# An adaLN block with linear attention and routed experts on one core: the ranking of a token group one head sooner, and the hand-over to the expert phase rearranged

## The reference

```python
def attn(x, w_qkv, w_out, b_out, proj):          # 4 x 1024 tokens, width 128, 8 heads of 16
    q, k, v = split(x @ w_qkv.T)                  # in blocks of 32 tokens
    qp = elu(q @ proj) + 1;  kp = elu(k @ proj) + 1      # 128 features for each head
    kv = kp.T @ v
    out = (qp @ kv) / (qp @ kp.sum(tokens) + 1e-8)       # within each block
    return out @ w_out.T + b_out

def ffn(x, w_red, wg, w1, b1, w2, b2):            # 8 experts, hidden width 512
    gates = softmax((x @ w_red) @ normalised(wg).T)
    idx, score = argmax(gates), max(gates)
    return (gelu(x @ w1[idx] + b1[idx]) @ w2[idx] + b2[idx]) * score

sa, ca, ga, sb, cb, gb = rows of silu(c) @ wmod          # ga, gb kept away from 0
h = layernorm(x) * (1 + ca) + sa;  x = x + ga * attn(h, ...)
h = layernorm(x) * (1 + cb) + sb;  x = x + gb * ffn(h, ...)
```

## Time and profile before

| | |
|---|---|
| three runs | 324.13, 325.55, 326.32 us, median 325.55 |
| profiled execution | 321.42 us, of which the span from the first to the last instruction is 319.7 |
| busy share of the span | PE 86%, DVE 74%, ACT 70%, POOL 49% |
| granted TensorE clock, mean | 0.949 of full speed |

### The profile page before, as it was taken

The page is one execution under the profiler, slowest core; times in us unless marked ns, Lnnn a source line. Parts: engine busy times, 40 slices in busy tenths (PEclk is TensorE's granted clock), DMA queues, the critical chain, the costliest instruction groups (busy, mean ns, idle before and its releaser), DMA issues. The chain is left out here.

```text
span 319.7 us, 11500 instructions
## 1 busy us (share of the span) xinstructions
PE 275.4 (86%) x4012; PEld 222.2 (70%) x4013; DVE 236.5 (74%) x769; ACT 224.2 (70%) x510; POOL 158.0 (49%) x173
## 2 busy tenths in 40 slices
PE   8789799999999999999999977684949699999960
PEld 3555577777777677687677756574849599999950
DVE  2767969989979989899899999595523456666740
ACT  1377788999889799889898689364237276676730
POOL 7104144362684774755746804557743434455550
PEclk9999999999999999999999999898578899999995
DMA  5996000000010011010100205134954424444400
GB/s 148 322 333 181 0 3 4 2 2 4 4 51 27 28 51 51 29 51 28 50 28 29 76 27 152 49 102 126 243 148 121 109 67 126 119 124 108 125 22 0
DMA packets 16240, 26.16 MB, mean 82 GB/s; under 512 B 2607, under 2 KB 11059, under 8 KB 16192
## 3 DMA queue, kind: packets, MB, share of 16 engines
q1 hardware_dynamic: 12464, 16.50, 18.8%
q0 software_dynamic: 3296, 8.41, 7.7%
q10 hardware_dynamic: 432, 0.59, 0.6%
HBM read 15.32 MB, written 10.64 MB: 81 GB/s over the span
## 5 line engine op out<-in xcount | busy, mean ns | idle before, releaser
L1129 DVE SCALAR_TENSOR_TENSOR phi<-ps,ebuf 128x512 f32<-128x512 f32 x128 | 82.0, 682 | 17.9 <-ACT ebuf L540 17.4
L536 ACT ACTIVATE ebuf<-ps 128x1024 f32<-128x1024 f32 x64 | 65.6, 1026 | 16.4 <-PE ps L766 15.6
L540 ACT ACTIVATE ebuf<-ebuf 128x512 f32<-128x512 f32 x128 | 74.4, 636 | 0.1
L764 PE MATMUL ps<-hT_hi,mix_lo 128*128 128x512 f32 x128 | 58.4, 456 | 8.2 <-DVE phi L1129 4.9
L594 ACT ACTIVATE gT<-ps,b_cols 128x128 f32<-128x128 f32 x156 | 44.7, 368 | 19.8 <-issue 13.6
L866 PE MATMUL ps<-w_sb,gT 128*128 x312 | 45.9, 294 | 13.2 <-DVE y L1446 11.3
L866 PEld LDWEIGHTS ps<-w_sb,gT 128*128 128x128 f32 x312 | 41.2, 206 | 15.2 <-issue 15.2
L766 PE MATMUL ps<-hT_hi,mix_hi 128*128 128x512 f32 x128 | 50.6, 396 | 0.0
L765 PE MATMUL ps<-hT_lo,mix_hi 128*128 128x512 f32 x128 | 50.6, 395 | 0.0
L495 POOL DMA_INDIRECT out<-yo,tok x27 | 27.4, 1014 | 29.7 <-issue 15.9
L446 POOL DMA_INDIRECT sorted_rows<-rec,pos x32 | 33.0, 1030 | 8.8 <-issue 5.4
(11 more groups left out here) (197 smaller groups left out, 452.5 us busy)
## 6 DMA issues: line engine op xcount, KB each, us to landing
rin<-sorted_rows SPq DMA_DIRECT2D x39, 192.5 KB
w1b<-in_L_ffn_w SPq DMA_DIRECT2D x1, 2048.0 KB, 14.2
sorted_rows<-pad_rec SPq DMA_DIRECT2D x6, 192.5 KB
sorted_rows<-pad_rec ACTq DMA_DIRECT2D x3, 192.5 KB
w1b<-in_L_ffn_b SPq DMA_DIRECT2D x1, 512.0 KB, 6.0
sorted_rows<-rec,pos POOLq DMA_INDIRECT x32
out<-yo,tok POOLq DMA_INDIRECT x27
wmod_sb<-in_L_wmod SPq DMA_DIRECT2D x1, 384.0 KB, 3.5
```

What stands on the lines that cost most here:

```text
L536: nc.scalar.activation(ebuf[:, h % 2, :, :], x_ps[h % 2], ACT.Relu, scale=-1.0).then_inc(s_neg, 1)
L540: nc.scalar.activation(ebuf[:, h % 2, j, :], ebuf[:, h % 2, j, :], ACT.Exp, scale=-1.0).then_inc(s_exp, 1)
L764: mm(x_ps[h % 2][:, j, :], mix_lo[:, j, h, :], hi, start=True, stop=False)
L1129: v.scalar_tensor_tensor(out=phi[:, h % 4, j, :], in0=x_ps[h % 2][:, j, :], scalar=0.0, in1=ebuf[:, h % 2, j, :], op0=ALU.max, op1=ALU.add ...
```

## The change

The ranking of group g-2 moves from head 7 to head 6 of step g, and for groups 0 to 5 into unused columns of PSUM bank 6, which `apply_values` of half 0 writes too. So it no longer waits for the residual (`s_x2`), the turning of the next group no longer waits for `s_pos`, and `apply_values` of half 0 waits for `s_cr` instead. In the last step the ranking of group 5 stands in head 5, the exponential of its gate in head 4, its score in head 5 and its positions in head 6. POOL scatters tile 0 of group 5 at the end of the last step and the other three one by one behind it. SP reads the row numbers of slots 12 to 17 one at a time, each just before or after a fetch. SP writes six paddings instead of five, and ACT two instead of three and one slot later. DVE adds the bias of slot 3 before the scores and positions of group 7 instead of behind them.

```diff
-    PADS_SP = E - 3
+    PADS_SP = E - 2
...
+        def rank_of(g):
+            return m_ps if isinstance(g, int) and g >= NG - 2 else ps[:, 6, TG * NC * VW:512]
...  (SP)
-            rows = [row_of(s) for s in range(EARLY, EARLY + RING)]
+            row = row_of(EARLY)
             sp.wait_ge(s_tail, 16 * (E + 1))
...
-            for s, row in zip(range(EARLY, EARLY + RING), rows):
+            for s in range(EARLY, EARLY + RING):
                 sp.wait_ge(f_yd, s - RING + 1)
                 fetch(s, row)
+                if s + 1 < EARLY + RING:
+                    row = row_of(s + 1)
...  (POOL)
                 if prev2:
                     build_scale(g - 2, firstp2)
+                if is_last(g):
+                    scatter(g - 2, [0])
                 if prev:
                     pool.wait_ge(s_ln2, 3 * g)
                     rsqrt(ln2_rs[:, :], ln2_ve[:, :], s_rs2)
...
             residual_base(NG - 1, False)
-            scatter(NG - 3, [0, 1])
+            scatter(NG - 3, [1])
             norm2_scale(NG - 2, False)
+            scatter(NG - 3, [2])
             pool.wait_ge(s_ln2, 3 * NG)
             rsqrt(ln2_rs[:, :], ln2_ve[:, :], s_rs2)
-            scatter(NG - 3, [2, 3])
+            scatter(NG - 3, [3])
...  (ACT)
-                    if h == 5 and prev2:
+                    if h == (4 if is_last(g) else 5) and prev2:
                         gate_exp(g - 2)
...
             gelu(5, 1)
-            act.wait_ge(s_table, 1)
-            for e in range(PADS_SP, E):
-                pad_region(act, e)
             for s in range(RING + 1, EARLY):
                 take_early(s)
                 keep_in(s, s)
                 gelu(s - 1, (s - 1) % 2)
+                if s == RING + 1:
+                    act.wait_ge(s_table, 1)
+                    for e in range(PADS_SP, E):
+                        pad_region(act, e)
...  (PE)
-                if is_last(g) and half == 1:
-                    pe.wait_ge(s_cr, NG - 1)
-                elif not first:
+                if half == 0 and g >= 2:
+                    pe.wait_ge(s_cr, g if g < NG - 1 else NG - 1)
+                if not first and not (is_last(g) and half == 1):
                     pe.wait_ge(s_on, 2 * g + half)
...
+                    if h == 5 and is_last(g):
+                        rank(g - 2)
...
-                    if h == 7 and prev2:
-                        pe.wait_ge(s_x2, g)
+                    if h == 6 and prev2 and not is_last(g):
                         rank(g - 2)
...  (DVE)
+                    if h == 5 and is_last(g):
+                        score_sum(g - 2)
+                        score_inverse(g - 2, firstp2)
...
+                        if h == 6:
+                            position_rows(NG - 3)
+                            position_own(NG - 3)
+                            position_sum(NG - 3)
+                            position_out(NG - 3, False)
...
+            add_bias(3, 3)
             scale_add(2, 2, 0)
             score_sum(NG - 1)
...
             position_out(NG - 1, False)
-            add_bias(3, 3)
```

More of the change, by code:

```diff
@@ L823, in rank @@
                 pe.wait_ge(s_pick, g + 1)
+                at = rank_of(g)
                 for t in range(TG):
                     for u in range(t + 1):
-                        mm(m_ps[:, t * E:(t + 1) * E], before[:, :] if u == t else ones_b[:, :], pick[:, u, :],
+                        mm(at[:, t * E:(t + 1) * E], before[:, :] if u == t else ones_b[:, :], pick[:, u, :],
                            start=(u == 0), stop=(u == t))
                 for t in range(TG):
-                    last = mm(m_ps[:, TG * E:(TG + 1) * E], ones_b[:, :], pick[:, t, :], start=(t == 0), stop=(t == TG - 1))
+                    last = mm(at[:, TG * E:(TG + 1) * E], ones_b[:, :], pick[:, t, :], start=(t == 0), stop=(t == TG - 1))
                 last.then_inc(s_rk, 1)
@@ L908, in step @@
                     if h == 2 and prev2:
-                        if not (isinstance(g, int) and g == 2):
-                            pe.wait_ge(s_pos, g - 2)
                         pe.wait_ge(s_x2, g - 1)
@@ L1258, in position_rows @@
                 dve.wait_ge(s_cr, g + 1)
-                v.tensor_tensor(posf[:, :, :], m_ps[:, 0:TG * E].rearrange("p (t e) -> p t e", e=E),
+                v.tensor_tensor(posf[:, :, :], rank_of(g)[:, 0:TG * E].rearrange("p (t e) -> p t e", e=E),
                                 carry[:, :].unsqueeze(1).broadcast_to([P, TG, E]), ALU.add).then_inc(s_ps, 1)
@@ L1264, in position_own @@
                 dve.wait_ge(s_ps, 2 * g + 1)
-                v.tensor_tensor(carry[:, :], m_ps[:, TG * E:(TG + 1) * E], carry[:, :], ALU.add).then_inc(s_cr, 1)
+                v.tensor_tensor(carry[:, :], rank_of(g)[:, TG * E:(TG + 1) * E], carry[:, :], ALU.add).then_inc(s_cr, 1)
                 v.tensor_tensor(posr3[:, :, :], posf[:, :, :], pick[:, :, :], ALU.mult).then_inc(s_ps, 1)
@@ L1318, in last_head @@
             def last_head():
-                position_rows(NG - 3)
-                position_own(NG - 3)
                 normalise_sum(NG - 1, 0)
-                position_sum(NG - 3)
                 normalise_inverse(NG - 1, 0)
-                position_out(NG - 3, False)
                 normalise_out(NG - 1, 0)
@@ L1388, in step @@
                         split_hi(g + 1, False)
+                    if h == 5 and is_last(g):
+                        score_sum(g - 2)
+                        score_inverse(g - 2, firstp2)
                     if h == 6:
-                        if prev2:
+                        if prev2 and not is_last(g):
                             score_sum(g - 2)
```

## The result

Four runs of the changed kernel took 328.89, 329.05, 329.49 and 333.00 us (median 329.27), four of the kernel before beside them 324.09 to 326.32 (median 324.84). The ratio is 1.018, 95% interval 1.013 to 1.023: slower by 4 to 7.5 us. The profiled execution took 329.49 us (span 327.7), 8.0 above the profiled one of before; the median difference is smaller since that execution of before was a quick one, as the prediction says.

The account below looks back on a forecast made before the run. The prediction saw a nearly full ring of PE, DVE and ACT, then SP's list in the hand-over. Terms 3.6 + 1.5 + 1.5 = +6.6 us on the median 325.55 gave 332, range 324 to 336.5.

Parts of the forecast that it names:

- part 1: Steps 3 to 7: PE waits 1.3 us for `carry` before half 0; 0.9 a step, +3.6 us (1.6 to 6.5).
- part 2: Last step: ranking of group 5 waits 2.8 us for `pick`; +1.5 us at the last count (0.5 to 4.3).
- the hand-over: Last count to the late slots: SP's sixth padding delays slot 9's fetch, +1.5 us (1.0 to 2.2).
- rival B: Ring absorbs the wait: part 1 at 1.6, perhaps part 2 low too; 329 to 330, or 328; chance 0.18.
- the ring: First-phase steps: PE, DVE and ACT hand work round, nearly full; PE leaves 0.9 us of a 22.3 us step.
- Rival D: Last step: PE's 2.8 us standstill could halve the clock, up to +1.7 us, 333.7; counted within the forecast's 0.46.
- Part 3: Hand-over: a sixth padding on SP before slot 9's fetch, +1.5 us (1.0 to 2.2).
- rival C: Queues get fuller: ACT stands 2 x 2.2 us for its paddings, part 2 nearer its upper end; +11, 336.5; chance 0.12.
- Part 4: Hand-over: earlier bias of slot 3, single row loads, sooner copy of slot 7's weights; at nothing, covered by SP's list.
- Rival A: Hand-over becomes quick: six paddings in 7.0 us, SP reaches slot 9 within 8 us; 325 or 322; chance 0.24.

Follow-up runs that it names:

- part 1 alone: Kernel before with only the steady steps' ranking in bank 6 and head 6, and half 0 of the applied values waiting for `carry`; ratio 1.0106.
- the trace of part 3: Kernel before with only six paddings on SP, two on ACT behind slot 7's gelu, and late slots' row numbers loaded one by one; ratio 0.997.
- parts 3 and 4 together: Kernel before with paddings 6 and 2, row numbers one by one, and slot 3's bias ahead of the last group's positions; ratio 1.0005.
- the repaired kernel: The whole change with group 5's ranking behind head 5's projection and scores, its positions at head 5's end; ratio 1.0075 against the kernel before.
- parts 3 and 4 each alone: Two runs on the kernel before: paddings 6 and 2 with row numbers one by one, 0.997; slot 3's bias ahead of the last positions, 1.0009.
- the outputs held back: Kernel before with POOL's output DMAs of the twelve early slots each waiting for a later slot than their own; ratio 0.9997.
- held back and spaced: Kernel before with early outputs held until all paddings landed and a small POOL operation of some 1.05 us behind each; ratio 1.0101.

## Why the prediction held, and where it did not

The direction and the range held: 332 was forecast, in 324 to 336.5, and 329.27 measured. That the sum came near is in part luck: between the two profiles it was +6.6 forecast and +8.0 measured, with part 1 1.6 too high, part 2 2.8 and the hand-over 1.2 too low, and 1.0 gained at start and end that nothing forecast. The measured time even lies just outside the forecast's own 329.5 to 335, in the 329 to 330 of rival B; of B the half on part 1 came true (+2.0 for its 1.6), the low end of part 2 did not. Point by point:

- **Part 1, the mechanism right, the size too large.** The wait came at the forecast place (1.37 for 1.3), and a step grew by 0.5, near the low end of 0.4, not by 0.9: +2.0 for four steps instead of +3.6. Of PE's 1.37 the ring swallowed 0.9, about PE's spare time in a step in the earlier trace rows. I had followed the delay only to DVE's head 2 and called the rest gapless; its gaps there were enough.
- **Part 1, the failed step.** "In the fifth, the last step, ACT waits 2.54 us [...] and that covers it" looked at step 7's first half 0. The same line of `apply_values` also runs for the last group behind head 7, where the wait is for `carry` of group 5. With part 1 alone PE stood there for 3.10 us, in the whole change for 1.26.
- **Part 2, undersized: +1.5 taken, +4.3 came**, the range's own upper end. The wait for `pick` (2.67 for 2.8) and DVE's wait for ACT (3.10 for 2.9) came as forecast. What I took off again did not: I counted on the 2.76 "remote" wait before the last sum to swallow the delay, and in its place stands a 2.67 wait for PE; PE itself ended late, by the half clock behind the first stop and by the second wait. Rival D's clock (up to +1.7) was real, about 3.5 us at half speed, and should have stood in the sum. The reason given for leaving it out was a misreading: the gap ahead of the slow window of the earlier trace rows was 2.57 us, not longer than the forecast stop of 2.8. A slip of the sum beside it: 3.4 less 2.76 leaves 0.64, not 0.9.
- **Part 3, the size plausible, the cause wrong.** I priced the sixth padding at 1.5 us between ACT's and SP's rows. Alone, it costs nothing. The Trainium skill ("DMA: Bandwidth & Descriptors", on issuing engines not being separate queues) has the split save only sequencer time; the trace of part 3 agrees in that the transfers cost the same, and even the sequencer's time did not show, since SP stood anyway. Of my two bounds the 2.2 was taken from SP under the hold-up and the 1.0 from ACT, which issued freely; neither was the price of one more padding in a list whose length the hold-up sets. That the queues were full, as the prediction reads these rows, is not what they show: ACT issued its two in 1.45 us while SP's were slow. So rival C's stand of ACT for 2 x 2.2 us did not come either.
- **Part 4, "at nothing", failed in company.** The earlier bias lets a sixth output be ready, which lengthens POOL's row by 1.3 us. With the sixth padding behind the row's end the late slots start 2.7 us later (3.0 in parts 3 and 4 together), but only 0.9 later in the repaired kernel, which has both parts too. By the times of parts 3 and 4 this cost at most 1.2.
- **Rival A** needed slot 9 within 8 us of the last count; it took 16.6. The quick list that it described exists (6.67 us for five paddings), but it needs POOL's outputs out of the way, and nothing in the change does that.

The parts add up: 1.06, 1.31 and 0.05 per cent make 2.4 where 1.8 was measured, within the intervals; by stretches of the trace +2.0, +4.3 and +2.7, less 1.0 at start and end, make the 8.0 of the two profiles.

## What to carry to other kernels

A wait that is added for a shared bank has to be looked up at every place where its line runs, the first and last iteration above all, and priced together with the list behind it: here the same ranking cost 1.3% ahead of the projection and nothing two places later. When several engines are released in the same microsecond by nothing that the profile names, look for a third engine whose row of DMAs ends just then, before pricing what they were waiting to do. Rows of indirect DMAs without a gap were worth breaking up here, but only from the start: held-back work came back as a row beside the late slots.

## What the runs showed of the hardware

- **Indirect DMAs in a row hold up the other engines.** While POOL issued them every 1.28 us (0.97 busy, 0.30 gap), SP's paddings took 2.2 us apiece, and signals of PE's finished work reached DVE and ACT late: DVE waited 7.67 us in before for an outer layer that PE had ended 6.1 us earlier, ACT 7.74 us in after. Rows of nine and ten ended at 234.71 and 241.93; SP was free at 236.1 and 243.6, DVE and ACT 1.5 to 2.0 us after the row's end. With one every 2.3 us (gap 1.3) behind the scatters the paddings took 1.4 apiece; with the four scatters alone, 1.3. In the late slots one every 2.0 us does no visible harm; eight in a row cost 9 us. How far SP gets before it slows down varies: behind the same row of nine the fetch of slot 9 came 13.9 to 14.1 us after the last count in four kernels with five paddings, and 15.0 in a fifth. The Trainium skill ("Perfetto Trace Analysis", section on the DMA instruction of GpSimd) says that such an instruction's end in the profile is the end of writing its descriptors, not of moving data; no row here shows where between the two the others are held, and no run tried a gap between 0.3 and 1.3 us.
- **The clock after a short stop is not the same from run to run.** Behind the same stop of PE (2.6 us before 204.3 and 204.7) matmuls went at half the clock for about 3.4 us in before and for about 10 us in the kernel with parts 3 and 4: granted clock by windows

```profile
210.00:215.00 5.00, 3.98 (x45) 3.69 (x45) 4.37 (x19) 3.56 (x13) 2.52 (x4) 1.00 0.46 129
```

```profile
210.00:215.00 5.00, 5.00 (x25) 5.00 (x25) 3.08 (x12) 2.07 (x8) 1.89 (x2) 0.50 0.39 122
```

(before above, parts 3 and 4 below; the clock is the third figure from the end). The last step came out at 48.6 and 50.7 us, and the whole difference arises between the `carry` of group 5 and that of group 6 (16.7 and 18.8 us), where the clock differs. It is the same in the other kernels with that stop: 3.4 us at half the clock and 16.7 in parts 3 and 4 each alone, 10 us and 18.8 with the outputs held back, and with them held back and spaced. Why one execution gets its clock back sooner stays open; parts 3 and 4 each alone were run on another chip of this type than the three with the long stretch, which is not excluded as the reason.
